# Row products of two graph layers: three BF16 matmuls against one in FP32

## What is computed

```python
h = x
for W, b in ((W1, b1), (W2, b2), (W3, b3)):       # 256->512, 512->512, 512->256
    g = h @ W
    msg = g[src] * norm_edge[:, None]             # dinv[src] * dinv[dst]
    h = relu(segment_sum(msg, dst, num_segments=n) + b)
return layernorm(x + h)
```

## Time and profile before

| | |
|---|---|
| Median of 3 runs | 2496.0 us (2494.5 to 2496.02) |
| The profiled execution's own time | 2488.2 us |
| Its span, first to last instruction | 2486.4 us |
| TensorE busy | 2271.8 us, 91% |
| POOL busy | 1753.4 us, 71% |
| VectorE busy | 1027.0 us, 41% |
| ScalarE busy | 521.7 us, 21% |
| DMA | 568.24 MB, 229 GB/s on the mean |
| Mean granted clock of TensorE | 0.965 |

### The profile page before, as it was taken

How to read it: one execution, slowest core, us unless ns; L and a number is a source line. 1 busy time by engine, 2 the same in 40 slices (tenths; PEclk the granted TensorE clock), 3 DMA queues, 4 the chain that set the end, 5 groups by cost and what they waited for, 6 DMA issues and landing times.

```text
span 2486.4 us, 42327 instructions
## 1 busy us (share of the span) xinstructions
PE 2271.8 (91%) x13351; PEld 1562.8 (63%) x13352; DVE 1027.0 (41%) x1307; ACT 521.7 (21%) x1322; POOL 1753.4 (71%) x1837
## 2 busy tenths in 40 slices
PE   6977799898999998999999999999988799999998
PEld 6855577676777773444444444444444688888887
DVE  8877333233333313444444444444422233333332
ACT  6611223222222312222222222222211000000000
POOL 5177777777777756777777777777776776767674
PEclk9788999999999999999999999999999899999999
DMA  6335666666666656888888888888887888888784
GB/s 215 119 118 184 222 203 206 201 198 205 192 209 190 208 170 204 253 272 268 267 264 264 263 267 264 264 268 258 275 260 236 261 257 249 252 248 255 245 247 140
DMA packets 231550, 568.24 MB, mean 229 GB/s; under 512 B 39868, under 2 KB 95795, under 8 KB 231475
## 3 DMA queue, kind: packets, MB, share of 16 engines
q0 software_dynamic: 126752, 399.62, 54.6%
q1 hardware_dynamic: 88371, 126.81, 14.5%
q10 hardware_dynamic: 16352, 40.77, 4.9%
HBM read 476.69 MB, written 90.36 MB: 228 GB/s over the span
## 4 chain that ended last, share of the span: by engine, by line
PE 55%; POOL 16%; issue 13%; DMA 7%; POOLq 4%; DVE 3%; ACT 0%; ACTq 0%; DVEq 0%; SPq 0%
POOL rows L671 16%; PE ps_acc L1511 9%; PE ps_h L1600 8%; PE ps_T L1600 7%; PE ps_o L1567 6%; DMA rows<-table,idx 5%; PE ps_d L1612 5%; PE ps_acc L1515 5%; PE ps_d L1515 4%; PE ps_h L1555 3%; PE ps_d L1511 3%; POOLq L680 3%; PE ps_d L1469 2%; DMA rows<-table_parts,idx 1%; PE ps_e L1588 1%
## 5 line engine op out<-in xcount | busy, mean ns | idle before, releaser
L671 POOL DMA_INDIRECT rows<-table,idx x912 | 870.0, 954 | 300.9 <-issue 264.7
L671 POOL DMA_INDIRECT rows<-table_parts,idx x884 | 837.1, 947 | 324.0 <-issue 268.2
L892 DVE SCALAR_TENSOR_TENSOR sel<-ps_e,firsts,dstT 128x1152 f32<-128x1152 f32 (+1 forms) x222 | 314.7, 1418 | 684.9 <-PE ps_acc L1511 253.9
L1515 PE MATMUL ps_acc<-rows,sel 128*128 128x512 f32 (+2 forms) x1122 | 489.8, 568 | 82.8 <-DMA rows<-table,idx 55.5
L1515 PE MATMUL ps_d<-rows,sel 128*128 128x512 f32 (+1 forms) x850 | 413.3, 616 | 41.3 <-DMA rows<-table,idx 41.2
L1511 PE MATMUL ps_acc<-rows,sel 128*128 128x256 bf16 (+1 forms) x2196 | 360.1, 280 | 50.5 <-DMA rows<-table_parts,idx 21.7
L1515 PEld LDWEIGHTS ps_acc<-rows,sel 128*128 128x128 f32 x1122 | 209.2, 202 | 250.0 <-issue 149.3
L1511 PEld LDWEIGHTS ps_acc<-rows,sel 128*128 128x128 bf16 x2196 | 217.9, 100 | 93.9 <-issue 37.8
L1515 PEld LDWEIGHTS ps_d<-rows,sel 128*128 128x128 f32 x850 | 152.8, 195 | 196.4 <-issue 119.2
L1567 PE MATMUL ps_o<-w,hT 128*128 128x512 f32 (+1 forms) x784 | 269.2, 486 | 1.2 <-ACT hT L1272 1.2
L1612 PE MATMUL ps_d<-parts,made_tiles 128*128 128x256 bf16 x1470 | 229.2, 272 | 0.5 <-issue 0.4
(11 more groups left out here) (190 smaller groups left out, 1902.8 us busy)
## 6 DMA issues: line engine op xcount, KB each, us to landing
built<-made_tiles SPq DMA_DIRECT2D x72, 384.0 KB
made_tiles<-built ACTq DMA_DIRECT2D x72, 384.0 KB
rows<-table,idx POOLq DMA_INDIRECT x912
rows<-table_parts,idx POOLq DMA_INDIRECT x884
table<-made SPq DMA_DIRECT2D x49, 256.0 KB
acc<-table SPq DMA_DIRECT2D x49, 256.0 KB
built<-made_tiles SPq DMA_DIRECT2D x24, 416.0 KB
made_tiles<-built ACTq DMA_DIRECT2D x24, 416.0 KB
```

Of the source, the lines that this page charges most:

```text
L671: pool.indirect_dma_start(out=to, out_offset=None, in_=its[0:nodes, :], in_offset=bass.IndirectOffsetOnAxis(ap=idx[:, of, k:k + 1], axis=0 ...
L892: v.scalar_tensor_tensor(to[:, k:k + FRONT, :], numbers.unsqueeze(1).broadcast_to([P, FRONT, P]), firsts[:, bass.ds(t, 1)], dstT[:, bass.d ...
L1515: return mm(to[:, 0:w], sel[:, k, :], rows_of[phase][:, k, 0:w] if first is None else first, start=start, stop=stop)
```

## The change

The three parts go. The dense blocks are copied from BF16 to FP32 on ScalarE, piece by piece, into a new tile `wide` (49 x 128 FP32 a partition). The table in SBUF is `whole` (49 x 256 FP32); `parts` had the room of both together. All row products of layers 1 and 3 become one FP32 matmul of 256 columns, in the gathered slots too, whose rows POOL now gathers from the FP32 tables. With them go `split_x` and `split` on VectorE, both stores of parts and POOL's wait for these. `wide` exists once: a piece of it is overwritten when TensorE has finished the same piece of the tile before (`dense_piece`), and TensorE waits for `widened`. In layer 3 the load of a later tile's piece is issued as soon as the piece has been widened.

In the last part of the diff, the first two hunks with `if` are the first lines and the end of a macro of layer 1 on ScalarE; then come layer 3's turns on ScalarE and two waits of POOL.

```diff
-        parts = sb("parts", [P, T, PARTS, C], BF16)
-        xs = parts[:, :, :, :].rearrange("p t i c -> p (t i c)")[:, 0:2 * T * C].bitcast(F32).rearrange(
-            "p (t c) -> p t c", c=C)
+        whole = sb("whole", [P, T, C])
+        xs = whole
+        wide = sb("wide", [P, T, P])
...
             def add_slot(to, phase, k, first, start, stop):
-                if in_parts:
-                    row = rows_parts[:, k, :] if first is None else first
-                    for i in range(PARTS):
-                        ins = mm(to[:, 0:C], sel_parts[:, k, :], row[:, i * C:(i + 1) * C],
-                                 start=start and i == 0, stop=stop and i == PARTS - 1)
-                    return ins
                 w = WIDTH[phase]
                 return mm(to[:, 0:w], sel[:, k, :], rows_of[phase][:, k, 0:w] if first is None else first,
                           start=start, stop=stop)
...
+            def wait_widened(q, h):
+                for piece, (lo_h, _) in enumerate(PIECES):
+                    if h == lo_h:
+                        pe.wait_ge(widened, len(PIECES) * q + piece + 1)
...
             def dense(i, into, hs):
                 j = 2 * i + into
                 for h in hs:
                     if h == 0:
-                        pe.wait_ge(blocks_in[into], 16 * len(PIECES) * (i + 1))
                         pe.wait_ge(dense_taken, j + 1)
-                    counts_of = blocks[into][:, h, :]
-                    for i in range(PARTS):
-                        ins = mm(ps_dense[into], counts_of, parts[:, h, i, :],
-                                 start=(h == 0 and i == 0), stop=(h == T - 1 and i == PARTS - 1))
+                    wait_widened(DENSE_1 + j, h)
+                    ins = mm(ps_dense[into], wide[:, h, :], whole[:, h, :], start=(h == 0), stop=(h == T - 1))
...
             def make(phase, t, s, per=1):
                 act.wait_ge(o_done, s + 1)
-                act.wait_ge(made_free, s + 1)
+                if phase == 1 and per == 1:
+                    to = whole[:, bass.ds(t, 1), :].rearrange("p a c -> p (a c)")
+                else:
+                    to = made[:, 0:w]
+                    act.wait_ge(made_free, s + 1)
...
+            def widen(q, of, pieces):
+                for piece in pieces:
+                    lo_h, hi_h = PIECES[piece]
+                    act.wait_ge(dense_piece, len(PIECES) * q + piece + 1)
+                    act.sem_inc(act_step, 1)
+                    nc.scalar.activation(wide[:, lo_h:hi_h, :], making[of][:, lo_h:hi_h, :], ACT.Copy).then_inc(widened, 1)
+            def widen_built(m, of, pieces):
+                act.wait_ge(self_added, m + 1)
+                widen(m, of, pieces)
...
                         if b == 0:
                             scale(0, t, t, s, 1)
                             scale_dense(m - 1)
+                            widen(m, 1 - of, range(len(PIECES) - 1, len(PIECES)))
                             keep_aggT(s, aggT[:, 0:C], 0)
...
+                    if build:
+                        widen_built(m + 1, of, range(len(PIECES) - 1))
...
+                def next_blocks(j, into, turn, more):
+                    act.wait_ge(blocks_in[into], 16 * len(PIECES) * (turn + 1))
+                    for piece in range(len(PIECES)):
+                        widen(DENSE_1 + j, into, [piece])
+                        if more:
+                            act.wait_ge(widened, len(PIECES) * (DENSE_1 + j) + piece + 1)
+                            load_blocks(j + 2, into, piece)
+                next_blocks(0, 0, 0, True)
                 deviation(0)
+                    next_blocks(j + 1, (j + 1) % 2, (j + 1) // 2, j + 3 < DENSE)
+                    deviations(j)
...
-                        if phase == 2:
-                            pool.wait_ge(parts_stored, 16 * (T - 1))
...
-                        pool.wait_ge(x_parts_stored, 16 * len(X_UNITS))
-                        window(0, MACRO, 1, need, in_parts=True, afresh=True)
```

More of the change, by code:

```diff
@@ L52 @@
 QUAD = 4
-PARTS = 3
 NONE = 255
@@ L564, in phases @@
                         rows_and_store(1, 0)
[L565 to L568, removed]
-                        with sp.Fori(len(X_DONE), MACRO) as t:
+                        with sp.Fori(2, MACRO) as t:
                             rows_and_store(t, t - 1)
@@ L685, in window @@
                 pool.sem_inc(pool_step, 1)
-                if need is None or afresh:
-                    gather(phase, 0, of, nodes, in_parts)
+                if need is None:
+                    gather(phase, 0, of, nodes)
                 else:
-                    gather_if(need, phase, 0, of, SLOTS, in_parts)
+                    gather_if(need, phase, 0, of, SLOTS)
                 for g in range(1, USED + 1):
@@ L1111, in macro @@
                         steady(0, MACRO + PER * m + b, (MACRO + PER * odd + b) % 2, hots,
-                               (m, place_of(m, True), of) if b == 0 else None, last=not build and b == PER - 1, in_parts=True)
+                               (m, place_of(m, True), of) if b == 0 else None, last=not build and b == PER - 1)
                 macro(0, 0, 0)
@@ L1128, in six @@
                                (q, place_of(q, False), u) if part == 2 else None)
-                        if not first or b > 0:
-                            split(t - 2)
-                six(0, True)
-                with v_.Fori(1, SIXES) as i:
+                with v_.Fori(0, SIXES) as i:
                     six(i)
@@ L1307, in tile @@
                     keep(PAIRS // 2, PAIRS)
-                make(phase, t, s)
+                make(phase, t, s, per)
             def keep_keys():
@@ L1516, in add_slot, with slots @@
                           start=start, stop=stop)
-            def slots(phase, n, ks, first, need=None, beside=None, ps=None, in_parts=False):
+            def slots(phase, n, ks, first, need=None, beside=None, ps=None):
                 to = ps_acc if ps is None else ps
@@ L1699, in beside @@
                                 n, wide = hi_h - lo_h, SLOTS - start
-                                dense_1(m, of, range(lo_h + (at - start) * n // wide, lo_h + (at - start + 1) * n // wide))
-                        steady(0, MACRO + PER * m + b, places, beside, s, in_parts=True, afresh=first and b == 0)
-                macro(0, 0)
+                                dense_1(m, range(lo_h + (at - start) * n // wide, lo_h + (at - start + 1) * n // wide))
+                        steady(0, MACRO + PER * m + b, places, beside, s)
+                pe.wait_ge(x_scaled[0], 4)
+                pe.wait_ge(x_scaled[1], 3)
+                macro(0)
                 with pe.Fori(0, DENSE_1 // 2 - 1) as i:
                     for u in range(2):
-                        macro(2 * i + u + 1, 1 - u)
-                macro(DENSE_1 - 1, 1, False)
+                        macro(2 * i + u + 1)
+                macro(DENSE_1 - 1, False)
                 turn(0, T - 2)
```

242 lines of the change are left out of this document (76 added, 166 removed).

## The result

The changed kernel takes 2721.6 us (median of 4 runs, 2720.1 to 2723.5) against 2495.3 us for the kernel before (4 runs): ratio 1.0911, 95% interval 1.0893 to 1.093. It is 9% slower. The forecast was 2743 us, 0.8% above. The time lies inside both of its ranges, in the narrower one (2720 to 2772 us) only just.

A forecast was written before the change was run, and what follows sets the result against it. TensorE was taken to bound layer 3 and layer 1's dense part, POOL layer 2. 2488.2 + 163 + 103 - 9.7 - 4 - 5.1 = 2735 us, 2743 by the median's ratio; range 2720 to 2772, wider 2715 to 2800.

The forecast's parts named there:

- Point 1: Layer 3: 24 windows of 65.9 row products, each 0.103 us dearer, +163 us; a window goes to 28.4 us.
- point 2: Layer 1: 490 dense and 508 slot row products, each 0.103 us dearer, +103 us, 10.3 us a macro.
- point 3: Layer 1, 300 to 428 us: TensorE's waits for rows fill with the longer matmuls, -9.7 us.
- Point 4: Layer 1, 130 to 300 us: VectorE's splitting of x, 25 stores and one gather go, -4 us (ends 0 and -8).
- Point 9: Layer 1's macro loop: 4.8 us of issue at each of three turns may shrink; taken as 0, other end -14 us.
- Point 6: Between layers 2 and 3: POOL no longer waits for the store of the parts, -5.1 us.
- Point 7: ScalarE's widening, 6.2 us a tile, stays hidden in layers 1 and 3: 0; far end +54 us.
- Points 5 and 8: Layer 2's splits and stores go under POOL's cover; dense loads are released earlier and gathers move fewer bytes: 0 each.
- less than the sum: Rival, chance 0.05: the loop's issue gap goes (-14) and layer 1's row waits absorb more; 2715 us or a little under.
- Widening on the path: Rival, chance 0.10: each of 34 tiles exposes one widening piece of ScalarE, +54 us, 2797 us.
- Loads in series: Rival, chance 0.01: weight load and stream add up, 0.406 us an FP32 record, +1247 us; about 3735 us.
- Not slower: Rival, chance 0.02: an FP32 matmul costs one pass, 0.216 us, so POOL binds layers 1 and 3; 2428 us.

The follow-up runs named there:

- experiment 3: Changed kernel with each dense product's FP32 matmul replaced by three BF16 matmuls, slots still FP32, dense sums left out: 2560.0 us, ratio 1.0272.
- experiment 1: Kernel before, with TensorE's loop over layer 1's macros written out, so no branch back: 2475.7 us, ratio 0.9938.
- Experiment 4: Changed kernel with each piece widened twice on ScalarE and both copies waited for: 2763.1 us, ratio 1.1087.
- Experiment 8: Kernel before with two BF16 matmuls a row product in place of three, third part left out of the sums, on a usual chip: 2428.7 us, ratio 0.9744.
- experiment 2: Changed kernel with four macros in TensorE's loop body in place of two: 2720.1 us, ratio 1.092.

## Why the prediction was right, and where it was off

The sum had 246.8 us, and 231.8 were measured (spans). By its points:

| Points | Forecast, us | Measured, us |
|---|---|---|
| 1, layer 3 | +163 | +162.5 |
| 2 to 4 and 9, layer 1 (with layer 2) | +89.3 | +71.5 |
| 6, between layers 2 and 3 | -5.1 | -2.2 |
| 5, 7, 8 | 0 | in the rows above |

- **Price of a row product** (+0.103 us): right. The dense runs give 0.2157 us a record against 0.2159 forecast, and experiment 3 finds the price in dense products and slots separately (0.103 and 0.107 us).
- **Weight loads** hidden: right. 1176 loads of 190 ns stand in each of the two dense groups, and records follow each other at 0.216 us. Loads and streams in series would be 0.406 us a record. The rule of the Trainium skill ("TensorE: Matmul & The Clock Gate", The mechanism), that a load overlaps matmuls in flight only when the row group differs, does not hold for these full 128 x 128 loads; the same section also has loads for a background weight buffer pulled ahead, and that agrees with the trace.
- **Point 1**: right, 28.5 us a window against 28.4. (6.9 us by 24 windows would be 165; from the 88th copy to the end it was 162.5.)
- **Points 2 and 3**: the two-macro body was forecast at 146 to 147 us and took 140.5 to 141.0. The first pass, which had no gap before it, grew by 18.1 us: 20.6 for the products, less 2.2 us of waits for rows that it had before. That is point 2 with its part of point 3. TensorE's passes begin at 363.7 us in both kernels, so the first macro's 10.3 us were paid by the rest of point 3 and by point 4 (forecast: 10.3 - 7.5 - 4 = -1.2 us). Point 3 took all of TensorE's waits for rows as filled, which was too much: of 7.9 us between 300 and 363.7 us, 4.5 are left in the changed kernel. That the first macro came out near all the same is in part luck, and no run parts the two points.
- **Point 4**: the eleventh copy of indices comes 4.6 us earlier (321.9 for 326.5 us), for which -4 was forecast. The mean gather in 130 to 300 us went from 0.995 to 129.81 / 133 = 0.976 us, not to 0.947. The traces say whose the slow ones were. Before, 25 gathers that run beside the splitting (L1009 to L1012) are 3.2 us longer than 0.946 us each would be, in all, and seven beside other work of VectorE 4.3 us. After, the 25 are gone and seven beside the same other work are left, with 5.1 us. Start, duration and work, two pairs of before and one of after:

```profile
217.68 1.12 POOL L671 DMA_INDIRECT rows<-table,idx  x1 [0.30 <-issue]
218.03 0.69 DVE L1011 CAST parts<-ps_d 128x512 bf16<-128x512 f32 x1
139.61 2.32 POOL L671 DMA_INDIRECT rows<-table,idx  x1 [0.30 <-issue]
138.57 2.55 DVE L946 TENSOR_TENSOR made_tiles<-late_ids,srcT 128x2304 bf16<-128x2304 int32 x1
...
133.23 3.18 POOL L627 DMA_INDIRECT rows<-table,idx  x1 [0.30 <-issue]
133.04 2.55 DVE L882 TENSOR_TENSOR made_tiles<-late_ids,srcT 128x2304 bf16<-128x2304 int32 x1
```

  So the splitting had 3.2 us of the 6.3 that the prediction gave as the far end. By the rule of the Trainium skill ("SBUF — State Buffer", the SWDGE trap), that a VectorE instruction in a two-port mode locks POOL out of writing descriptors, all 6.3 us would go only if nothing but the splitting did it. The traces agree in that every slow gather runs beside work of VectorE (in which mode, they do not say), and show that 4.3 us of 7.5 stood beside other work.
- **Point 9 is the step that failed.** It took the 4.8 us of issue at a turn of the loop as staying, at 0, with -14 as the other end. They went at all three turns, 15.4 us by TensorE's idle time in the two traces; taking the gap alone out of the kernel before gave 16.7 us (experiment 1). With -16 in its place the sum is 2719 us against 2720.1 measured; that they meet so closely is in part luck, since points 3 and 6 were off as well. The mechanism was named (a shorter body) and the value was taken from the wrong side. The row that spoke for the other end was there: layer 3's loop, with the shorter body, had no gap. Its branch takes 0.21 us.
- **Point 6**: -2.2 in place of -5.1. POOL's pause at 1921 us is gone: gathers follow each other at 1.25 us through 1997 to 2002 us. But the pause was not what the time hung on. The chain passes, in both kernels, through the product of layer 2's last tile and the landing of its row in the table (before, before, after; the last two lines of the fence are POOL's, after):

```profile
1933.50 5.30 DMA table<-made
1938.89 1.62 DMA table_parts<-parts
2004.46 3.84 DMA table<-whole
...
1997.12 0.95 POOL L627 DMA_INDIRECT rows<-table,idx  x1 [0.30 <-issue]
1998.38 0.95 POOL L627 DMA_INDIRECT rows<-table,idx  x1 [0.30 <-issue]
```

  What the change saves there is the landing of the parts and a shorter landing of the row, 5.30 + 1.62 - 3.84 = 3.1 us, of which 2.2 us are left at the 88th copy. The prediction had the right store and the wrong wait for it.

- **Point 7**: right, 6.0 us a tile and no wait of TensorE for it. "A few tenths" of lateness did not show. Experiment 4 shows how thin the cover is in layer 1 and how thick in layer 3. So the rival with a chance of 0.10 was not far off in layer 1: at twice the price the widening was on the path.
- **Points 5 and 8**: right. Layer 2 runs at 1.26 us a gather as before. DMA moves 490 MB in place of 568 and nothing gets faster by it.

The rivals: *less than the sum* came about in its first half, the gap; its other half (more waits for rows filled) did not, so the time is 2721.6 and not below 2715. It is nearer to this rival's 2715 than to the forecast's 2743 all the same, though the rival had a chance of 0.05 only. *Widening on the path*: falls, for this kernel. *Loads in series*: falls by the record spacing. (Its 3735 us leave out the savings that its text takes off: 2488 + 1247 - 19 = 3716 us.) *Not slower*: falls, two records a matmul. Experiment 8 puts a number on its far side: with TensorE's work cut by a third, POOL binds layer 3 at 19.9 us a window, for which the rival had 20.2.

How the branch depends on the body was shown in five kernels. By the instruction records of TensorE (loads, matmuls and its sequencer's) that I counted in one pass: fast (0.21 us) at about 1530 and at 1510 to 1550 records, slow (3.8 to 4.9 us) at about 1725, 1935 and 3059. That it is the length and not the type of the matmuls follows from experiments 2 (FP32, slow) and 8 (BF16, fast).

The traces also show what goes with a slow branch. The profile counts packets of instructions on a DMA queue of their own, q8. From the first turn of the loop to the branch that leaves it, before (486.6 to 864.5 us) and then after (504.7 to 927.8 us):

```profile
q1 hardware_dynamic: 9504, 18.29, 13.7%
q8 instruction: 20, 0.33, 0.3%
...
q1 hardware_dynamic: 9504, 18.29, 11.9%
```

Before, 20 packets of 16 KB; after, no line of q8: the body's instructions came in once, six packets during the first pass, and none after. Experiment 8 has none either, experiment 3 has 13, and experiment 2, where only TensorE's loop was edited, has 20 between 504.7 and 927.8 us, so the queue is TensorE's. At each of the seven slow branches of the three kernels one packet of q8 begins 1.4 to 2.5 us after the branch does. Written out (experiment 1) the instructions come in just the same, 21 packets from 486.6 to 840 us, and no gap appears. So what costs is a jump back to instructions that have to be brought in again; that the branch waits for that one packet fits all seven, but is not in the trace as a wait.

## What to carry to other kernels

Count an FP32 matmul by its records in the trace before trading BF16 parts for it: here it is two records of about twice a BF16 matmul's time each, so nearly four against three (0.432 against 0.329 us), and the copies, stores and bytes that it saves are worth nothing where another engine covers them. A gap of issue at a loop's turn is a cost of its own, which an edit of the body's length can take away or bring back; compare it with a shorter loop of the same kernel, look for instruction packets in later passes, and try the loop written out. A pause of an engine is worth what it is worth on the chain: here 5.1 us of POOL's gave 2.2. An engine with much idle time on the average may still have a margin of a microsecond or two at the place where its work is wanted: double the suspected work to measure it.

## What the runs showed of the hardware

- A backward branch of TensorE's weight-load sequencer took 0.21 us with bodies up to about 1550 records and 3.8 to 4.9 us from about 1720 on. TensorE went on for 16 or 17 records in each of the seven cases and was then idle: 4.5 to 5.5 us where the records were BF16 of 0.11 us, 2.15 us where they were FP32 of 0.216 us, 3.2 to 3.9 us where they were mixed.
- With bodies up to about 1550 records no packet of instructions moved on q8 in the later passes; with 1720 and more they did (13 and 20 packets of 16 KB).
- The same kernel took 2492 to 2496 us on some chips and 3082 to 3085 us on two others. Stretches bound by TensorE took the same time there (28.5 us a window), with a clock of 1.00; in layer 2 a gather left every 1.53 us in place of 1.25, and part of the waits of POOL and others had a "remote" releaser. On such a chip the change cost 1.4% in place of 9%.
- On the usual chips an indirect gather of 128 rows left every 1.25 us whether a row has 1024 bytes (layer 3 after), 1536 (layer 3 before) or 2048 (layer 2).
- A gather took 1.0 to 3.2 us in place of 0.946 beside some instructions of VectorE: 25 beside the splitting of x (3.2 us in all), seven beside others (4.3 and 5.1 us).
- ScalarE's copy from BF16 to FP32 took 1.48 us for 1536 elements a partition and 1.59 us for 1664.
